# Query and key weights in eight plain pieces, cast by three engines, and eight row buffers at the start of a fused attention and expert kernel

## The reference, cut to what matters

```
xn = (x - mean) / sqrt(var + 1e-5)
q  = xn @ q_w.T + q_b
xd = depthwise conv (3 taps, stride 2) of xn along tokens, + conv_b     # 1024 rows
k  = xd @ k_w.T + k_b ;  v = xd @ v_w.T + v_b
att = softmax(q k^T / 8) v  (16 heads of 64) ;  attn = att @ out_w.T + out_b
e  = argmax(xn @ W_router)  ;  y = gelu(xn @ W1[e] + b1[e]) @ Wo + bo + xn
out = x + attn + layernorm(y)
```

## Time and profile before

| | |
|---|---|
| median of 3 runs | 1967.33 us (1964.52 to 1977.75) |
| the profiled execution | 1971.07 us; its slowest core (3) spans 1969.5 us |
| spans of the 8 cores | 1947.0 to 1969.5 us |
| PE busy, of the span of core 3 | 1828.8 us (93%) |
| DVE, ACT, POOL busy | 934.0, 895.2, 298.3 us |
| DMA | 366.69 MB |
| mean granted PE clock of core 3 | 0.981 |

### The profile page before, as it was taken

How to read it: one execution, slowest core, us unless ns; L and a number is a source line. 1 busy time by engine, 2 the same in 40 slices (tenths; PEclk the granted TensorE clock), 3 DMA queues, 4 the chain that set the end, 5 groups by cost and what they waited for, 6 DMA issues and landing times.

```text
span 1969.5 us, 37041 instructions; the slowest of 8 cores (1947.0 to 1969.5 us)
## 1 busy us (share of the span) xinstructions
PE 1828.8 (93%) x12540; PEld 1004.3 (51%) x12540; DVE 934.0 (47%) x1257; ACT 895.2 (45%) x1381; POOL 298.3 (15%) x357
## 2 busy tenths in 40 slices
PE   3588999998999999887899999999999999999995
PEld 1245222232554222222566666766666676666663
DVE  3354689856563888774132233413333323332225
ACT  2244988887455977775122222322222322222221
POOL 3122001001230110011001111101111111101111
PEclk9799999999999999998999999999999999999998
DMA  7759989984686999954756566856555776556551
GB/s 172 182 150 122 181 159 172 162 156 144 183 174 138 141 167 169 166 184 156 260 195 216 203 213 215 266 207 218 211 204 186 249 263 212 183 188 208 203 197 72
DMA packets 89171, 366.69 MB, mean 186 GB/s; under 512 B 11792, under 2 KB 11936, under 8 KB 68000
## 3 DMA queue, kind: packets, MB, share of 16 engines
q1 hardware_dynamic: 50112, 252.06, 38.8%
q0 software_dynamic: 38880, 112.27, 29.7%
HBM read 363.27 MB, written 94.90 MB: 233 GB/s over the span
## 4 chain that ended last, share of the span: by engine, by line
PE 73%; DMA 10%; DVE 6%; ACT 6%; issue 3%; POOL 0%; SPq 0%; DVEq 0%; ACTq 0%; POOLq 0%
PE ff_py L981 25%; PE ff_pu L946 25%; ACT pbuf L556 5%; DMA xa_d<-stg 4%; PE ps_a L505 4%; PE ps_s L543 4%; PE ps_a L569 4%; PE ps_q L367 3%; DMA row<-x 3%; DVE rc L581 3%; PE ps_q L395 2%; PE ps_m L574 2%; PE ps_q L381 2%; DMA xn_d<-row 2%; DMA stg<-x 1%
## 5 line engine op out<-in xcount | busy, mean ns | idle before, releaser
L960 ACT ACTIVATE ff_it<-ff_pu,b1t 128x256 bf16<-128x256 f32 (+1 forms) x608 | 244.3, 453 | 729.6 <-PE ff_pu L946 729.6
L556 ACT ACTIVATE pbuf<-ps_s 128x1024 bf16<-128x1024 f32 x512 | 477.3, 1061 | 116.8 <-PE ps_s L543 99.4
L946 PE MATMUL ff_pu<-ff_xg,ff_w 128*128 128x256 bf16 (+1 forms) x4864 | 516.4, 265 | 1.1 <-DVE ff_xg L930 1.1
L981 PE MATMUL ff_py<-ff_wo,ff_it 128*128 128x512 bf16 x2240 | 510.7, 381 | 3.8 <-DVE stg L511 3.8
L946 PEld LDWEIGHTS ff_pu<-ff_xg,ff_w 128*128 128x128 bf16 x4864 | 444.9, 98 | 73.4 <-issue 1.3
L981 PEld LDWEIGHTS ff_py<-ff_wo,ff_it 128*128 128x128 bf16 x2240 | 218.7, 98 | 238.2 <-issue 8.1
L581 DVE RECIPROCAL rc<-ps_m 128x512 f32<-128x512 f32 x64 | 214.7, 3355 | 44.9 <-PE ps_m L574 44.2
L569 PE MATMUL ps_a<-pbuf,v_sb 128*64 128x512 bf16 x1024 | 209.1, 404 | 5.8 <-DVE masks_all L464 4.8
L543 PE MATMUL ps_s<-qT,kT 64*128 64x512 bf16 x1024 | 201.3, 384 | 11.9 <-ACT pbuf L556 9.7
L574 PE MATMUL ps_m<-pbuf,ones 128*64 128x512 bf16 x1024 | 197.7, 381 | 0.0
L930 DVE COPY ff_xg<-ff_pt 128x1024 bf16<-128x1024 bf16 x35 | 24.2, 691 | 348.0 <-PE ff_pt L923 348.0
(11 more groups left out here) (135 smaller groups left out, 1238.7 us busy)
## 6 DMA issues: line engine op xcount, KB each, us to landing
ff_w<-scrW SPq DMA_DIRECT2D x152, 1024.0 KB
scrW<-w POOLq DMA_DIRECT2D x64, 512.0 KB, 15.6
row<-x SPq DMA_DIRECT2D x32, 512.0 KB, 6.6
xn_d<-row SPq DMA_DIRECT2D x32, 512.0 KB, 5.8
row<-xn_d SPq DMA_DIRECT2D x32, 512.0 KB, 15.8
stg<-x SPq DMA_DIRECT2D x32, 512.0 KB, 12.1
xa_d<-stg SPq DMA_DIRECT2D x32, 512.0 KB, 8.9
scrWo<-wo POOLq DMA_DIRECT2D x16, 512.0 KB, 13.0
```

The costliest lines, as they stand in the source:

```text
L556: e_at[g] = op("scalar", lambda s: s.activation(pbuf[g % 4][:, :], ps_s[g % 2][:, :], AF.Exp, scale=0.125), w)
L946: E.emit("tensor", lambda t, r_=r, q_=q, ic_=ic, c=cc, j_=j, sl=k % NW1SLOT: t.matmul(pu[r_][:, q_, 0:n], w1[:, sl, c * 512 + ic_ * 128:c ...
L960: E.emit("scalar", lambda s, r_=r, q_=q, ic_=ic, i_=i, j_=j, k_=k: s.activation(it[:, k_ % 3, ic_, 0:n], pu[r_][:, q_, 0:n], AF.Gelu, bias ...
L981: E.emit("tensor", lambda t, a_=a, o=oh, ic_=ic, i_=i, k_=k: t.matmul(py[:, 2 * a_ + o, :], it[:, k_ % 3, ic_, a_ * 128:(a_ + 1) * 128], w ...
```

## The change

The query and key weights are packed on the host in eight pieces of 512 KB each (half h of the output columns, pair c of input chunks). SP loads each piece plain, in float32, into a staging area (`qwf`, `kwf`) with a semaphore for each piece. `cast_w` then writes the bfloat16 weight: piece i on DVE, ACT or POOL by i mod 3. The query staging lies over the later value and key weights, so the value load and the casts of the key weight wait for all query casts; the key staging lies over `v_sb` and the output weight, so the output load waits for the key casts.

The first eight tiles have eight row buffers (four more in memory that is used only later), so their loads wait for nothing. SP's order is now: tiles 0 to 3, query pieces 0 to 3, tiles 4 and 5, query pieces 4 to 7, tiles 6 and 7, all eight key pieces, and only then the stores of tiles 0 to 3. From tile 8 on there are four buffers in turn, as before.

The query casts stand ahead of the first group; `a_stats` of tiles 4 to 7 moves to q 0 (groups 0, 1, 3, 5), `a_norm` of tiles 4 and 5 to q 0 (2, 3), the transposes of block 1 to q 0 (4, 6, 7) and q 1 (0). The key casts hang on q 1, one for each group, the convolution of block 0 moves from q 0 to q 1. The value load moves from q 1, group 0 to q 0, group 4. A q or k group waits for the casts of its half of the weight.

```diff
-    row = [place(f"row{i}", [128, D], F32, O_ROWS + i * 4 * KB) for i in range(4)]
+    row = [place(f"row{i}", [128, D], F32, o) for i, o in enumerate(
+        [O_ROWS + 4 * KB * k for k in range(4)] + [O_STG + 4 * KB * k for k in range(3)] + [O_OTP + 12 * KB])]
...
+    def load_piece(name, dst, src, i):
+
+        piece[name, i] = dma("sync", lambda s: s.dma_start(
+            dst[:, i * 1024:(i + 1) * 1024], src[i, :, :]), sWP[name][i])
+
+    def cast_w(name, dst, src, i, waits=()):
+
+        h, c = divmod(i, 4)
+        to = dst.rearrange("p (c d) -> p c d", c=CC)[:, 2 * c:2 * c + 2, h * 512:(h + 1) * 512]
+        of = src[:, i * 1024:(i + 1) * 1024].rearrange("p (c d) -> p c d", c=2)
+        eng = ("vector", "scalar", "gpsimd")[i % 3]
+        if eng == "scalar":
+            m = op(eng, lambda s: s.copy(to, of), [piece[name, i]] + list(waits))
+        else:
+            m = op(eng, lambda e: e.tensor_copy(to, of), [piece[name, i]] + list(waits))
+        W[name][h].append(m)
...
     def a_load(gt):
-        s_ = ring["n"] % 4
-        ring["n"] += 1
+        if gt < NT:
+            s_ = gt % 8
+        else:
+            s_ = ring["n"] % 4
+            ring["n"] += 1
...
     for t in range(4):
         a_load(t)
-    W["q"] = load_w(qw, qwT_d, sWQ)
+    for i in range(8):
+        if i == 4:
+            a_load(4)
+            a_load(5)
+        load_piece("q", qwf, qwT_d, i)
+    a_load(6)
+    a_load(7)
+    for i in range(8):
+        load_piece("k", kwf, kwT_d, i)
     a_stats(0)
-    for t in range(6):
-        if t >= 2:
-            a_transpose(t - 2, (5, 7)[t % 2])
+    for t in range(4):
         if t < 3:
             a_stats(t + 1)
-        if t >= 4:
-            a_stats(t)
         a_norm(t)
-        if t < 4:
-            a_load(t + 4)
-    W["k"] = load_w(kw, kwT_d, sWK, [W["q"]])
+        if t:
+            a_transpose(t - 1, (5, 7)[(t - 1) % 2])
+    a_transpose(3, 7)
+    for i in range(8):
+        cast_w("q", qw, qwf, i)
...
+    for t in range(4):
+        later(todo, ("q", 0, (0, 1, 3, 5)[t]), lambda t_=t: a_stats(4 + t_))
     for t in range(2):
-        later(todo, ("q", 0, t), lambda t_=t: a_stats(6 + t_))
-    for blk, tr, nrm in ((1, (("q", 0, 1), ("q", 0, 3), ("q", 0, 5), ("q", 0, 7)), None),
+        later(todo, ("q", 0, t + 2), lambda t_=t: a_norm(4 + t_))
+    for i in range(8):
+        later(todo, ("q", 1, i), lambda i_=i: cast_w("k", kw, kwf, i_, q_cast))
+    for blk, tr, nrm in ((1, (("q", 0, 4), ("q", 0, 6), ("q", 0, 7), ("q", 1, 0)), None),
...
-        for blk, at in ((0, ("q", 0, c)), (1, ("k", 0, c)), (2, ("q", 2, c)), (3, ("q", 3, c))):
+        for blk, at in ((0, ("q", 1, c)), (1, ("k", 0, c)), (2, ("q", 2, c)), (3, ("q", 3, c))):
...
-    later(todo, ("q", 1, 0), lambda: next_w("v", vw, vwT_d, sWV, "k"))
-    later(todo, ("k", 1, 0), lambda: next_w("o", ow, owT_d, sWO, "v"))
+    later(todo, ("q", 0, 4), lambda: next_w("v", vw, vwT_d, sWV, q_cast))
+    later(todo, ("k", 1, 0), lambda: next_w("o", ow, owT_d, sWO, W["k"][0] + W["k"][1] + [W["v"]]))
```

More of the change, by code:

```diff
@@ L60, in packT, with pieces @@
         return f(w.T.reshape(CC, 128, D).transpose(1, 0, 2).reshape(128, CC * D))
-    d["qwT"] = packT(np.asarray(inputs["L0_attn_q_w"], np.float32))
-    d["kwT"] = packT(np.asarray(inputs["L0_attn_k_w"], np.float32))
+    def pieces(w):
+        return f(w.T.reshape(4, 2, 128, 2, 512).transpose(3, 0, 2, 1, 4).reshape(8, 128, 1024))
+    d["qwT"] = pieces(np.asarray(inputs["L0_attn_q_w"], np.float32))
+    d["kwT"] = pieces(np.asarray(inputs["L0_attn_k_w"], np.float32))
     d["vwT"] = packT(np.asarray(inputs["L0_attn_v_w"], np.float32))
@@ L131, in build_nc @@
     out_d = nc.dram_tensor("out", [NTOK, D], F32, kind="ExternalOutput").ap()
-    qwT_d, kwT_d, vwT_d, owT_d = [din(n, [128, CC * D]) for n in ("qwT", "kwT", "vwT", "owT")]
+    qwT_d, kwT_d, vwT_d, owT_d = [din(n, s) for n, s in (
+        ("qwT", [8, 128, 1024]), ("kwT", [8, 128, 1024]), ("vwT", [128, CC * D]), ("owT", [128, CC * D]))]
     qb_d, kb_d = din("qb", [128, CC]), din("kb", [128, CC])
@@ L154, in build_nc @@
     sCONST, sCAST, sCASTO, sROW, sRT, sRT2 = [mksem(n) for n in ("sCONST", "sCAST", "sCASTO", "sROW", "sRT", "sRT2")]
-    sWQ, sWK, sWV, sWO, sWR, sVB = [mksem(n) for n in ("sWQ", "sWK", "sWV", "sWO", "sWR", "sVB")]
-    sX = [mksem(f"sX{i}") for i in range(4)]
-    sXN = [mksem(f"sXN{i}") for i in range(4)]
+    sWV, sWO, sWR, sVB = [mksem(n) for n in ("sWV", "sWO", "sWR", "sVB")]
+    sWP = {n: [mksem(f"sWP{n}{i}") for i in range(8)] for n in "qk"}
+    sX = [mksem(f"sX{i}") for i in range(8)]
+    sXN = [mksem(f"sXN{i}") for i in range(8)]
     sSTL = [mksem(f"sSTL{i}") for i in range(3)]
@@ L190, in build_nc @@
     mtmp = sb("mtmp", [128, NT], F32)
-    lst = sb("lst", [128, 4, 12], F32)
-    lmv = sb("lmv", [128, 4, 2], F32)
-    lrs = sb("lrs", [128, 4, 4], F32)
+    lst = sb("lst", [128, 8, 12], F32)
+    lmv = sb("lmv", [128, 8, 2], F32)
+    lrs = sb("lrs", [128, 8, 4], F32)
     mhalf = sb("mhalf", [128, 2], F32)
@@ L257, in load_w @@
         return dma("gpsimd", lambda g: g.dma_start(dst[:, :], src[:, :]), sem, waits)
-    W = {}
-    ring = {"n": 0, "free": [[], [], [], []], "xnb": [[], []]}
+    W = {"q": [[], []], "k": [[], []]}
+    piece = {}
+    def load_piece(name, dst, src, i):
[11 more added lines that the diff above has]
+        W[name][h].append(m)
+    ring = {"n": 0, "free": [[] for _ in range(8)], "xnb": [[], []]}
     tile_in = {}
@@ L369, in q_group @@
                 start=(c == 0), stop=(c == CC - 1)),
-                ([W["q"], xnt_at[gb]] + K.bank[r]) if cc == 0 else [], inc=cc == CC - 1)
+                (W["q"][oc // 4] + [xnt_at[gb]] + K.bank[r]) if cc == 0 else [], inc=cc == CC - 1)
         q_last[gb] = m
@@ L383, in k_group @@
                 start=(c == 0), stop=(c == CC - 1)),
-                ([W["k"], conv_m[gb]] + K.bank[r]) if cc == 0 else [], inc=cc == CC - 1)
+                (W["k"][oc // 4] + [conv_m[gb]] + K.bank[r]) if cc == 0 else [], inc=cc == CC - 1)
         kv_last["k", gb] = m
@@ L604, in attention @@
                 for t in range(3):
+                    stg_free[t] = stg_free[t] + ring["free"][4 + t]
                     load_out_x(b * NT + t)
```

7 lines of the change are left out of this document (5 added, 2 removed).

## The result

In the first timing, whose chip isn't on record, the changed kernel took 1981.75 us (median of 20 executions), the kernel before 1964.84 us (20). The quotient of these medians is 1.0086; the ratio on record is 1.0059 with a 95% interval of [1.0038, 1.0081]. The forecast of 1961 us was 21 us too low and its range ended at 1975. Run again without a change on chips 10, 10 and 13, the kernel gave 1.0019 [0.9997, 1.0041], 0.9995 [0.9981, 1.0009] and 0.9999 [0.9977, 1.0022]. So there are two things to explain: why a gain of 6.3 us in the first stage became nothing, and why the first timing made it a loss.

A forecast was written before the change was run, and what follows sets the result against it. The first projection was taken to wait for row loads slowed by whole-matrix weight loads beside them. 89.8 - 76.0 - 5.0 - 2.5 = 6.3 us off 1971.07 gave 1964.8, less 3.7 over the median 1961 us; range 1947 to 1975.

The forecast's parts named there:

- a gain of 6.3 us in the first stage: First sequence's projection: 89.8 - 76.0 - 5.0 - 2.5 = 6.3 us earlier at k 1, and so at the end.
- tile 8 at 76.0: Row load in the first projection, thirty-fourth 512 KB transfer: lands at 76.0 us against 89.8, 13.8 us earlier.
- k 0 near 89: Key groups of block 0 in the first projection, waiting for statistics of tiles 8 to 11: start near 89 us.
- k 1 near 106: Key groups of block 1 in the first projection: start near 106 us, where the kernel before had 112.15.
- The last `v_sb`: Value output ending the first projection, behind which attention begins: near 193.5 us instead of 200.0.
- q 1: Query groups of block 1 in the first projection: end near 62 us, where the kernel before had 89.7.
- The first matmul: First query matmul on PE in the first projection: near 20 us instead of 34.9.
- Core 3 is the slowest: All sums are for core 3; the change is worth what it moves the start of attention, at 200.0 us there.
- take 200.0 - 112.15 for the rest, unchanged: From the start of k 1 to attention: same steps in the same order, so the same time, 88 us.
- (c): DMA queue: each transfer pays part of a fixed cost; tile 8 at 96.6 us, 14 us slower, 1982 us; chance 0.06.
- (b): DMA queue: all cores stream at once, 1.89 us a transfer; tile 8 at 85.9, 3.6 us slower, 1971 us; chance 0.16.
- (d): Start of k 0: it doesn't wait for tile 11, so 20 to 27 us gained, 1944 us; chance 0.06.

The follow-up runs named there:

- e_after: The changed kernel run again unaltered on chip 10: 1966.91 us, 1.0019 of the kernel before.
- f_after: The changed kernel run again unaltered, a second time on chip 10: 0.9995 of the kernel before.
- g_after: The changed kernel run again unaltered on chip 13: 0.9999 of the kernel before.
- c_odd: The changed kernel with one 2 MB scatter of the query weight behind the value load, written on odd cores only, chip 8: 1.0005 of the kernel before.
- u_both: The changed kernel with both weights by the old casting transfers, eight row buffers and new order kept, chip 10: 1964.84 us, 0.9996 of the kernel before.
- f_order: The changed kernel with statistics of tiles 8 to 11 and two normalizations moved to v 0, repeated on chip 10: 0.9892 of the kernel before.
- c_all: The changed kernel with one 2 MB scatter of the query weight behind the value load, written on all eight cores, chip 8: 1.0022 of the kernel before.
- d_order: The changed kernel with statistics of tiles 8 to 11 and two normalizations moved to v 0, chip 8: 1948.70 us, 0.9891 of the kernel before.
- a_all: The changed kernel with two 2 MB scatters ahead of the first attention, written on all eight cores, chip 1: 1.0170 of the kernel before.
- b_fast: The kernel before with two 2 MB scatters ahead of the first attention, written on cores 1, 2, 5, 6, chip 1: 1.0124 of the kernel before.
- d_odd: The changed kernel with the order of d_order and a 2 MB scatter on odd cores, chip 8: 1950.90 us, 0.9914 of the kernel before.

## Why the prediction was wrong, step by step

Up to k 1 the walk through the stage was right for its core. Forecast and found on core 3: tile 8 at 76.0, found 76.95; k 0 near 89, found 89.48; k 1 near 106, found 106.21. The last `v_sb` was to be done near 193.5 instead of 200.0, and was at 195.6 (194.88 + 0.69): 89.4 us behind k 1 where the prediction had 88, so 4.4 us of the 6.3 were left there. q 1 ended at 57.4 instead of 62: the groups ran with fewer gaps than I had allowed for, and a cast on DVE took 0.69 us and not 1.0. The first matmul came at 23.72 instead of 20. Both lie in front of the wait for tile 8 and cost or bring nothing. The queue took 8.51 MB in 25 us, 1.54 us for 512 KB, and then 1.68 beside the value weight (6.96 MB in 63.6% of 35 us), where the sum had 1.60 throughout. The rule weighed against the pieces, at least 1 MiB for a transfer (the Trainium skill, DMA: Bandwidth & Descriptors, Bandwidth), is not borne out by that row for a queue that is kept full.

**The step that failed** is in the first paragraph: "Core 3 is the slowest, and all sums below are for it. From 200 us on the program is the same; so the change is worth what it moves that point." With it goes the end of the third, "take 200.0 - 112.15 for the rest, unchanged". They failed in four ways. The numbers below are from one profiled execution of each kernel, so tenths of them can be chance.

- *One late core stood for all.* Much of what the change moved on core 3 was the gap between the cores of a pair. It showed in the profile of before, had I read k 0 or `v_sb` on all eight cores: four were 7 to 10 us earlier. A full queue on every core at once puts all of them at k 0 at 88 to 90 us. At k 1 the four late cores gained 6.7 us and the four early ones 0.7, 3.7 in the mean. Nor was core 3 the slowest by this stage: cores 4 and 7 came to attention later (201.8 and 202.2 us) and ended earlier (1961.8 and 1963.3 us). It spent 312.2 us from the first scores of the second sequence to the feed-forward stage, where the other seven spent 303.0 to 307.0; after the change it spent 304.1. That stretch, which no step of the prediction looks at, is the larger part of the 13.3 us that its span lost.
- *From k 1 to attention the time did change.* It was 86.7 us before and 89.2 in `e_after` in the mean of the cores (89.6 and 89.8 in `f_after` and `g_after`), 2.4 of the 3.7 us. In `c_odd`, whose pairs are apart, it was 87.9. This would fit with the cores of a pair slowing each other's output weight when they load it at once; it isn't shown.
- *From attention on the same program took longer.* The first attention takes 287.1 us on nearly every core in place of 286.1 (and 287.1 in `u_both` too, so it comes with the buffers or the order, not with the pieces; by what, wasn't found). The second projection takes 139.6 us in the mean in place of 138.7, as four cores took 137.9 before; the second attention gives 0.7 back. The feed-forward stage took 1030.2 us in the mean of the eight cores before, 1032.1 in `e_after`, 1033.2 in `f_after`, 1031.9 in `f_order`, 1031.8 in `c_all`, and 1030.7 in `c_odd`, whose pairs are apart again. That would fit with cores of a pair being in each other's way when in step; but `u_both`, with pairs 1.3 to 6.8 us apart, has 1032.0, so it isn't shown. Together: 1.2 gained, 0.8 + 0.8 - 0.7 + 1.9 given back, and the mean span of the eight cores went from 1956.8 to 1958.5 us. Over all executions the pairs' later core has a median span of 1961.5 and 1962.0 us after against 1960.2 and 1960.8 before on chip 10, and the mean core 1958.9 and 1958.8 against 1956.4 and 1957.3.
- *In the first timing, the clock of that same program.* A fall to 0.81 in at least one pair turned 1965 into 1980 us in three executions of four; the four without one ended at 1964.7 to 1967.7, where the kernel before has 1964.84. So this is the whole difference between 1.0059 and 1.000, and no rival named it.

Of the rivals, (c) and (b) name times near the first result, 1982 and 1971, and neither is what happened: tile 8 landed at 76.95, not at 96.6 or 85.9. Rival (d), a gain of 20 us or more if k 0 doesn't wait for tile 8 to 11, is wrong for this kernel and is just what `d_order` makes true: 19 us at attention, 20 at the end against the changed kernel on chip 10 (1946.29 and 1965.84 us) and 21 against the kernel before on chip 8. The chances had 0.85 on within 1%, and the ratio lies there each time. That is little credit, as no gain of the 6.3 us arrived; the time's range ended too low, for it had no term for the clock or for what later stages do to a gain.

## What to carry to other kernels

Read the point that a change moves on every core before pricing it on the slowest: the slowest may only be the late one of a pair, or slow by a stage that the change doesn't touch, and here a change that filled the queue evened the cores out instead of moving them all. A stretch of the same program is not a stretch of the same length: check the one behind the last sum too. Then ask what the next wait hangs on in the order of the engine that serves it; here four statistics placed one stage too early cost 20 us, and with the buffers and pieces in place moving them was worth 1% where those alone had brought nothing. And time a change of half a per cent on more than one chip before believing its sign, and count clock falls in the profile, not by means.

## What the runs showed of the hardware

- A granted clock of 0.81 held by the two cores of a pair for 161 or 162 us (first timing, `a_all`, `b_fast`) while other cores of the same die ran dense matmuls at 1.00; for 3 to 6 us in profiles of chips 8 and 10, 40 to 60 us on chip 13, and 1090 us and more in `d_odd`. TensorE: Matmul & The Clock Gate (Part 1) of the Trainium skill has a limiter to 13/16 that takes the whole die once three of its cores run dense matmuls, as long as the load lasts. The level agrees with the 0.81 of the rows; that it takes a die and stays doesn't: core 3 had 0.98 to 1.00 in the stretches in which core 0 had 0.78 to 0.81. Here it took a pair in all profiles but `d_order`'s, where all four cores of a die had it for 4 to 5 us, and it ended under full load. The two pairs of the die in `d_odd` had it at different times, together only from 1011 to 1118 us.
- A pass that casts 128 x 1024 from float32 to bfloat16 takes 0.69 us on DVE, where I had 1.0.
- A scatter in which no row is written still took 21.9 to 23.7 us from issue to landing on the even cores of `c_odd`, where the same one writing 2 MB took 30.9 to 31.2 on the odd cores.
